# Loading the convolution's image by upper and lower halves, in pieces of ten full rows, in place of halves by columns

## The reference, cut to what matters

```python
h = einsum('oc,bchw->bohw', w1, x)          # 48 -> 288 channels ("expand")
h = relu(bn(h, g1, b1, m1, v1))
h = conv_3x3_depthwise(h, wd, padding=1)    # each channel by itself
h = relu(bn(h, gd, bd, md, vd))
h = einsum('oc,bchw->bohw', w2, h)          # 288 -> 48 ("project")
h = bn(h, g2, b2, m2, v2)
return x + h
```

## Time and profile before

| what | us |
|---|---|
| median of 3 runs | 2143.0 (2142.28, 2143.00, 2147.72) |
| the profiled execution | 2147.49 |
| its span, first to last instruction | 2145.7 |
| attention | to about 855 |
| MLP | about 856 to 1220 |
| convolution | about 1220 to the end |

### The profile page before, as it was taken

How to read it: one execution, slowest core, us unless ns; L and a number is a source line. 1 busy time by engine, 2 the same in 40 slices (tenths; PEclk the granted TensorE clock), 3 DMA queues, 4 the chain that set the end, 5 groups by cost and what they waited for, 6 DMA issues and landing times.

```text
span 2145.7 us, 75224 instructions
## 1 busy us (share of the span) xinstructions
PE 2012.5 (94%) x29192; PEld 1624.2 (76%) x29192; DVE 1464.3 (68%) x2586; ACT 1368.1 (64%) x2839; POOL 673.1 (31%) x874
## 2 busy tenths in 40 slices
PE   5999999999999997689999799998999899999996
PEld 4777777777777776445555489888989888888985
DVE  4899999998999997545555555554655556565553
ACT  2777777777777775456666466665666566665664
POOL 3233323333233332903200243343333332425240
PEclk9999999999999998799999899999999999999999
DMA  1222222222222221566655262635444445445331
GB/s 59 63 67 69 66 69 70 67 69 66 69 70 66 69 67 63 118 153 152 149 134 133 60 142 70 128 85 117 111 102 111 109 83 136 91 116 111 90 98 31
DMA packets 286411, 198.71 MB, mean 93 GB/s; under 512 B 225975, under 2 KB 275656, under 8 KB 276472
## 3 DMA queue, kind: packets, MB, share of 16 engines
q1 hardware_dynamic: 282850, 189.17, 35.1%
q0 software_dynamic: 2336, 6.20, 1.2%
q10 hardware_dynamic: 1014, 0.34, 0.1%
HBM read 128.31 MB, written 54.72 MB: 85 GB/s over the span
## 4 chain that ended last, share of the span: by engine, by line
PE 53%; ACT 2%; DVE 2%; issue 1%; DMA 1%; SPq 0%; ACTq 0%; DVEq 0%
PE psum L1063 13%; PE psum L1082 12%; PE psum L1115 9%; PE psum L664 6%; PE psum L649 5%; PE psum L1123 5%; PE psum L638 3%; ACT h2T L1151 1%; DMA room<-tok_mid 1%; DVE h L848 0%; DVE room L680 0%; SPq L600 0%; ACT h L847 0%; DVE room L848 0%; DVE room L693 0%
## 5 line engine op out<-in xcount | busy, mean ns | idle before, releaser
L897 POOL TENSOR_TENSOR mats<-mats,dscale 112x2048 f32<-112x2048 f32 x72 | 260.8, 3622 | 483.4 <-DMA mats<-in_taps 480.5
L1063 PE MATMUL psum<-ew,xp 64*100 64x96 f32 x6144 | 318.3, 251 | 24.6 <-DVE h L848 11.1
L1151 ACT ACTIVATE h2T<-psum 96x1024 f32<-96x1024 f32 x192 | 195.7, 1019 | 202.4 <-PE psum L1123 202.4
L848 DVE TENSOR_SCALAR h<-psum 100x384 f32<-100x384 f32 x384 | 211.8, 557 | 155.7 <-PE psum L1063 138.7
L1063 PEld LDWEIGHTS psum<-ew,xp 64*100 64x100 f32 x6144 | 290.8, 165 | 34.6 <-DVE h L848 15.8
L1082 PE MATMUL psum<-h,mats 128*64 128x128 f32 x4608 | 273.1, 278 | 11.7 <-issue 10.1
L1082 PEld LDWEIGHTS psum<-h,mats 128*64 128x64 f32 x4608 | 256.8, 139 | 21.2 <-issue 12.1
L847 ACT ACTIVATE room<-psum 64x512 f32<-64x512 f32 (+1 forms) x384 | 206.1, 537 | 93.6 <-PE psum L1082 87.2
L344 PE MATMUL psum<-kb,qa 128*64 128x256 f32 x2048 | 251.7, 388 | 2.2 <-DMA kb<-kk 2.2
L848 DVE TENSOR_SCALAR room<-psum 64x512 f32<-64x512 f32 (+1 forms) x288 | 174.2, 605 | 80.5 <-PE psum L1082 74.6
L1115 PE MATMUL psum<-h2T,pw 128*64 128x128 f32 x3072 | 209.2, 278 | 17.7 <-ACT h2T L1151 17.7
(11 more groups left out here) (155 smaller groups left out, 3436.8 us busy)
## 6 DMA issues: line engine op xcount, KB each, us to landing
mats<-in_taps SPq DMA_DIRECT2D x69, 896.0 KB, 6.2
tok_mid<-mid SPq DMA_DIRECT2D x128, 224.0 KB, 1.9
room<-tok_mid SPq DMA_DIRECT2D x64, 448.0 KB, 3.7
piece<-img_mid SPq DMA_DIRECT2D x196, 63.8 KB, 2.4
img_mid<-room SPq DMA_DIRECT2D x128, 97.5 KB, 2.7
kb<-kk SPq DMA_DIRECT2D x512, 24.0 KB
out<-yc SPq DMA_DIRECT2D x32, 384.0 KB, 4.3
scratch<-in_x_tokens SPq DMA_DIRECT2D x126, 96.0 KB, 1.9
```

The lines of the kernel that those rows point to most:

```text
L848: return nc.vector.tensor_scalar(dst, src, 0.0, None, ALU.max)
L897: nc.gpsimd.tensor_tensor(m, m, bc(scale[0:MROWS, at:at + TCH], 2, POUT), ALU.mult).then_inc(mats_scaled, 1)
L1063: mm = nc.tensor.matmul(ring[(j + u) % 4][0:PIN, p:4 * CH:4], xp[hx][rows, 2 * j + p, :], w1[rows, c, :], start=True, stop=True)
L1151: nc.scalar.activation(h2T[n % 2][0:CH, :, :], ps_t[0:CH, :, 0:POUT * PART], ACT.Copy).then_inc(copied, 1)
```

## The change

The image is halved by rows: a half is 64 full rows, its upper 32 on partitions 0 to 47 and its lower 32 on partitions 64 to 111. `PC, PR = 16, 4` (now for each side) gives the same 64 patches a side. A piece is ten full rows of 130 columns, so each channel's part is one run of 5200 bytes, and there are four pieces and eight DMAs a half, in two slots. A cut writes 16 patches. The borders are cleared on all partitions by three memsets. A step's eight patches lie beside one another, so the add into `y` writes eight runs of eight pixels in eight rows. `y` is 32 rows of 128 pixels and lies in `room`. It is stored to an output that is in image order already. The last layer's bias comes in as a row of `w2` against a row of ones in `h2T`, so `c2` goes with its loads and folding; its loads for `b` and `m` are made for `q`. The tiles' total work in multiplications is the same. The diff, cut:

```diff
-PC, PR = 8, 16
-PATCHES = PC * PR
+PC, PR = 16, 4
+PATCHES = 2 * PC * PR
 MROWS = 112
-HALF = PC * PW
-SC = HALF + 2
+ROWS = PH * PR
...
-        q = {n: sb(f"q_{n}", [CH, C]) for n in "gvt"}
-        c2 = {n: sb(f"c_{n}", [P, 1]) for n in "gbmvt"}
+        q = {n: sb(f"q_{n}", [CH, C]) for n in "gbmvt"}
...
-        SLOTS = 5
-        SIDE = HALF // 2 + 2
+        SLOTS = 2
...
-        piece = [sb(f"piece{s}", [P, PH + 2, SIDE]) for s in range(SLOTS)]
+        piece = [sb(f"piece{s}", [P, PH + 2, W + 2]) for s in range(SLOTS)]
...
-        y = sb("yc", [P, PR * PH, PC // 2 * PW])
+        y = room[:, PATCHES // 2 * CH:PATCHES // 2 * CH + ROWS * W].rearrange("q (r x) -> q r x", x=W)
+        mark = sb("mark", [1, 1])
...
-        STEPS = [(pc, a, PART) for a in range(0, PR, PART) for pc in range(PC // 2)]
+        STEPS = [(j, c) for j in range(PR) for c in range(0, PC, PART)]
...
-            slot, _ = place_of(j)
-            src = piece[slot][:, :, :]
-            src = bass.AP(src.tensor, src.offset, [list(src.ap[0]), [PW, PC // 2], [SIDE, PH + 2], [1, PW + 2]])
-            dst = xp[hx][:, :, :].rearrange("k (c j) (r x) -> k j c r x", j=PR, x=PW + 2)[:, j]
+            src = piece[j % SLOTS][:, :, :]
+            src = bass.AP(src.tensor, src.offset, [list(src.ap[0]), [PW, PC], [W + 2, PH + 2], [1, PW + 2]])
+            dst = xp[hx][:, PC * j:PC * j + PC, :].rearrange("k c (r x) -> k c r x", x=PW + 2)
...
         def close_borders(pool, hx, h):
...
-            if hx == 0:
-                last = nc.gpsimd.memset(ones(0)[:, 0, :, :, 0], 0.0)
-            else:
-                last = nc.gpsimd.memset(ones(1)[:, PC // 2 - 1, :, :, PW + 1], 0.0)
-            last.then_inc(border_set, 1)
-            pool.wait_ge(border_set, 2 * h + 1)
-            for r in range(2):
-                nc.gpsimd.memset(ones(r)[:, :, 0, 0, :], 0.0)
-                last = nc.gpsimd.memset(ones(r)[:, :, PR - 1, H - PH * (PR - 1) + 1:, :], 0.0)
-            last.then_inc(border_set, 1)
+            at = xp[hx][:, :, :].rearrange("k (j c) (r x) -> k j c r x", c=PC, x=PW + 2)
+            edge = at[0:ONE, 0, :, 0, :] if hx == 0 else at[ONE:P, PR - 1, :, PH + 1, :]
+            for n, t in enumerate((at[:, :, 0, :, 0], at[:, :, PC - 1, :, PW + 1], edge)):
+                nc.gpsimd.memset(t, 0.0).then_inc(border_set, 1)
+                pool.wait_ge(border_set, 3 * h + n + 1)
...
+        def load_piece(eng, b, hx, j, done):
+
+            for r in range(2):
+                top = 2 * ROWS * hx + ROWS * r + PH * j - 1
+                lo, hi = max(top, 0), min(top + PH + 2, H)
+                eng.dma_start(piece[j % SLOTS][ONE * r:ONE * r + C, lo - top:hi - top, :], d["img_images"][:, b, lo:hi, :])\
+                    .then_inc(done, 16)
...
-            constants = [(t[...], 0.0) for t in (w1, w2, *c2.values(), *h2T, *piece, *xp)]
+            constants = [(t[...], 0.0) for t in (w1, w2, *h2T, *piece, *xp)]
             constants += [(t[96:P, :, :], 0.0) for t in mats]
+            constants += [(t[CH:P, :, :], 1.0) for t in h2T]
...
-            loads += [(q[n][:, :], d[f"bn2_{n}"].partition_broadcast(CH)) for n in "gv"]
-            loads += [(c2[n][r:r + C, :], d[f"bn2_{n}"].rearrange("(c a) -> c a", a=1)) for n in "gbmv" for r in (0, ONE)]
+            loads += [(q[n][:, :], d[f"bn2_{n}"].partition_broadcast(CH)) for n in "gbmv"]
             loads += [(dn[n], d[f"{n}d"].partition_broadcast(MROWS)) for n in "vgmb"]
-            assert len(loads) == 24
+            assert len(loads) == 18
...
-            nc.gpsimd.memset(y[:, 0:H // 2, :], 0.0).then_inc(y_stored[0], 32)
-            pool.wait_ge(y_stored[0], 32)
-            nc.gpsimd.memset(y[:, H // 2:H - PH, :], 0.0).then_inc(y_done, 1)
-            pool.wait_ge(y_done, 1)
-            nc.gpsimd.memset(y[:, H - PH:H, :], 0.0).then_inc(y_stored[1], 32)
-            pool.wait_ge(y_stored[1], 32)
+            for n, (done, value) in enumerate(((y_stored[0], 32), (y_stored[1], 32), (y_done, 1))):
+                nc.gpsimd.memset(mark[:, :], 0.0).then_inc(done, value)
+                pool.wait_ge(done, value)
...
-                slot, nth = place_of(j)
-                wait(pool, cut, nth)
-                lo, hi, off = piece_rows(j)
-                for r in range(2):
-                    pool.dma_start(piece[slot][ONE * r:ONE * r + C, off:off + hi - lo, :],
-                                   d["img_images"][:, 0, lo:hi, HALF // 2 * r:HALF // 2 * r + SIDE]).then_inc(first_loaded, 16)
+                wait(pool, cut, j - SLOTS + 1)
+                load_piece(pool, 0, 0, j, first_loaded)
...
-            nc.scalar.activation(c2["t"][:, :], c2["v"][:, :], ACT.Sqrt, bias=eps[:, :]).then_inc(root, 1)
...
+            nc.vector.tensor_tensor(w2[CH:CH + 1, CHUNKS - 1, 0:C], q["b"][0:1, :], q["m"][0:1, :], ALU.subtract)
+            for t in (e, dn):
...
             def load_half(b, hx, h):
 
                 for j in range(PR):
-                    slot, nth = place_of(j)
-                    wait(sp, cut, PR * h + nth)
-                    lo, hi, off = piece_rows(j)
-                    for r in range(2):
-                        x0 = HALF * hx + HALF // 2 * r
-                        sp.dma_start(piece[slot][ONE * r:ONE * r + C, off:off + hi - lo, :],
-                                     d["img_images"][:, b, lo:hi, x0:x0 + SIDE]).then_inc(piece_loaded[slot], 16)
+                    sp.wait_ge(cut, PR * h + j - SLOTS + 1)
+                    load_piece(sp, b, hx, j, piece_loaded[j % SLOTS])
...
-                        rows = slice(PH * PART * block, PH * PART * (block + 1))
+                        rows = slice(ROWS // 2 * block, ROWS // 2 * (block + 1))
                         for r in range(2):
-                            sp.dma_start(d["out"][4 * b + 2 * hx + r].rearrange("c (y x) -> c y x", y=H)[:, rows, :],
+                            at = 2 * ROWS * hx + ROWS * r
+                            sp.dma_start(d["out"][b].rearrange("c (y x) -> c y x", y=H)[:, at + rows.start:at + rows.stop, :],
...
             def add(n, b, hx, c, k):
 
-                pc, a, m = STEPS[n]
+                j, first = STEPS[n]
                 dve.wait_ge(y_ready, NSTEP * k + n + 1)
-                rows = slice(PH * a, PH * (a + m))
-                cols = slice(PW * pc, PW * pc + PW)
-                dst = y[:, rows, cols]
-                src = ps_y[n % 2][:, 0:POUT * m].rearrange("q (r x) -> q r x", x=PW)
+                view = lambda t: t.rearrange("q (p r x) -> q p r x", p=PART, x=PW)
+                dst = y[:, PH * j:PH * j + PH, PW * first:PW * (first + PART)].rearrange("q r (p x) -> q p r x", x=PW)
+                src = view(ps_y[n % 2][:, :])
                 if c == 0:
                     if n % PER_BLOCK == 0:
                         dve.wait_ge(y_stored[n // PER_BLOCK], 32 * (2 * b + hx) + 32)
-                    p0 = PR * pc + a
-                    x = xp[hx][:, p0:p0 + m, :].rearrange("k j (r x) -> k j r x", x=PW + 2)[:, :, 1:PH + 1, 1:PW + 1]
-                    nc.vector.tensor_tensor(dst.rearrange("q (j r) x -> q j r x", j=m),
-                                            src.rearrange("q (j r) x -> q j r x", j=m), x, ALU.add).then_inc(y_done, 1)
-                elif c == CHUNKS - 1:
-                    nc.vector.scalar_tensor_tensor(dst, src, c2["b"][:, 0:1], dst, ALU.add, ALU.add).then_inc(y_done, 1)
+                    x = xp[hx][:, PART * n:PART * n + PART, :].rearrange("k p (r x) -> k p r x", x=PW + 2)[:, :, 1:PH + 1, 1:PW + 1]
+                    nc.vector.tensor_tensor(dst, src, x, ALU.add).then_inc(y_done, 1)
                 else:
                     nc.vector.tensor_tensor(dst, src, dst, ALU.add).then_inc(y_done, 1)
...
-    d["out"] = nc.dram_tensor("out", (B * 4, C, H * HALF // 2), F32, kind="ExternalOutput").ap()
+    d["out"] = nc.dram_tensor("out", (B, C, H * W), F32, kind="ExternalOutput").ap()
     block_program(nc, d)
     got = run_bass_kernel_spmd(nc, [arrays], core_ids=[0]).results[0]["out"]
-    return got.reshape(halves).transpose(0, 3, 4, 1, 2, 5).reshape(B, C, H, W)
+    return got.reshape(B, C, H, W)
```

More of the change, by code:

```diff
@@ L788, in conv @@
         LEAD = 3
-        BLOCKS = PR // PART
+        BLOCKS = 2
         PER_BLOCK = NSTEP // BLOCKS
@@ L801, in more @@
             return not (hx == 1 and isinstance(b, int))
[L803 to L817, removed]
+        FIXED = 2 + 2 + SLOTS + 2 + LOADS + 2 + 2 + 2 * SLOTS
+        PER_SLOT = PR // SLOTS
         def number(b, hx, c):
@@ L955, in _ @@
                 for j in range(PR):
-                    slot, _ = place_of(j)
-                    pool.wait_ge(piece_loaded[slot], 32 * (PER_HALF[slot] * (h - 1) + nth_in_slot(j) + 1))
-                    if j:
-                        pool.wait_ge(cut, PR * h + j)
-                    else:
-                        pool.wait_ge(border_set, 2 * h)
+                    pool.wait_ge(piece_loaded[j % SLOTS], 32 * (PER_SLOT * (h - 1) + j // SLOTS + 1))
```

(16 more changed lines are left out.)

13 lines of the change are left out of this document (2 added, 11 removed).

## The result

The changed kernel took 2162.2 us in the median of 5 runs (2158.3 to 2166.1), against 2143.2 for the kernel before: a ratio of 1.0084, with an interval of 1.0064 to 1.0104. It is 18 us slower by the ratio and 19 by the medians, where 2 us less was forecast, and 2162 lies above the range of 2134 to 2149. The profiled execution took 2158.3, a span of 2156.5, so the two traces differ by 10.8 us: the execution profiled before was near the slow end of its runs, this one at the fast end. I read the places from the traces and the size from the medians.

What follows compares the result with a forecast made beforehand. TensorE, busy for 94% of the span, was taken to bound the kernel. Terms of -1.0, -0.06, -0.5, -0.2 and -0.2 made -2.0, from a median of 2143.0 to 2141.0 us, range 2134 to 2149.

Steps and rivals of the forecast that it cites:

- the term "-1.0" for the transfers of the pieces: First chunks of halves that load pieces: fewer, longer transfers shorten TensorE's waits slightly, -1.0 us.
- -4.7 (or -8.0): Lower bound for piece transfers: first chunks fall to the last half's excess of 1.13 us; -8.0 includes h6.
- rival 2: First chunks of halves that load pieces: long runs hold up PE's instruction loads, +8.3 us, 2150; chance 0.10.
- Rival 1: First chunks: the piece packets are the stall, so these fall to the last half's level, -8.0 us, 2134; chance 0.10.
- Rival 3: MLP's start: the crowd of loads dissolves, token wait and slow stretch vanish, -8.1 us, 2133; chance 0.06.
- the term of -0.2 for POOL's loads: MLP's start: six small loads fewer, tap loads about 1.4 us sooner, same bytes; -0.2 us, bounds -8.1 and +2.
- Rival 4: Piece transfers: not shortened, as 48 runs are handled worse than 112, but hidden; 2142 us, chance 0.06.
- The signs that I had named: Whole kernel: some 120,000 fewer small packets, quiet chunks 36.36, h6's wait near 2 us, cuts 2.1 us, no POOL waits.
- rival 2's sign: First chunks of halves: above 40 us with a granted clock under 1.00.
- The constants at the MLP's start: POOL's memsets before the MLP: the second xp memset ends 0.6 us earlier; -0.5 us taken, bounds -0.8 and +0.5.
- SP, POOL, adds, bias: Convolution: SP and POOL cost 0 on the path, bias nothing, only the very last add counts, -0.06 us.

Runs made afterwards that it cites:

- its best version: Changed kernel with late pieces, taps and stores of y in four DMAs each, POOL's two early tap loads behind the first half's cuts: 2133.4 us, 0.9938.

## Why the prediction was wrong

**The step that failed** is the term "-1.0" for the transfers of the pieces; it is about +18, which is what the medians give back when the pieces come late (2165.1 to 2147.0), or 16 by the ratios. Its bounds were -4.7 (or -8.0) on one side and rival 2 on the other, which ends at 2150. In its place the runs showed: dummy loads alone bring the 18 us, leaving the pieces out takes them away, and the wait is PE's, put down to "issue", behind an instruction packet that comes late. Rival 2 had the place (first chunks of the halves that load pieces), the sign and the means (PE's instruction loads), but my price, each odd half raised to h6's excess, was too low, and it named the wrong property: long runs. Neither ten times shorter runs (2169) nor DMAs of a tenth of the bytes (2155) cure it.

**What misled me** was right as far as it went. I read that h6's wait came when no piece packet had moved, and concluded that most of the stall belongs to taps and store. That is right for h6: with split taps its excess goes from 4.4 to 0.4, with the pieces late only to 3.3. For h1 and h3 it is not: either change alone nearly clears them, so their stall took both (the changed kernel without pieces keeps 0.9 and 0.8 us there). And even "the old pieces have no part in the old stall" wouldn't say that the new ones add nothing to it. PE already waited in each first chunk, so there was no slack left there, and any new traffic at that place goes straight onto the path. I had counted the pieces' engine time, 14.1 against 8.4 us a half, which did fall (384 runs of 365 ns are 8.8); what counts here is what the engines hold at the moment when a load is due. Then 0.65 MB were queued at once before (ten DMAs) and 1.0 MB after (four DMAs of 250 KB), and half the queue or smaller DMAs each bring back some 9 us.

**Rival 1** (2134, the piece packets are the stall) didn't come: the transfers got shorter and the stall longer, and without any pieces the time is only that of the kernel before. As a reading of the old trace it holds for h1 and h3 in part, and not for h6. **Rival 3** went the other way. In the profiled execution the waits for tokens were 3.28 and 2.89 us, 6.2 in all for 5.8, but in the other 12 traces with the changed kernel's MLP they were 10.6 to 12.3, against 5.8, 7.1 and 9.5 in the three of the kernel before and its versions. The convolution starts at 1234.8 to 1236.3 us in these three and at 1235.7 to 1240.6 in the 13, at 1239.0 in the middle one. So the term of -0.2 for POOL's loads, bounded at +2, is by these traces nearer to +4. The version with late pieces, 0.8 us above before in the median, leaves little room for as much in the medians, and why the same two tap loads, issued at nearly the same time, make PE wait longer there stays open. **Rival 4** is wrong as well; the transfers did get shorter.

**The signs that I had named** were mixed. Quiet chunks of 36.36, h6's wait near 2 us (1.85), and no wait of PE for POOL came as said; the cuts were quicker (1.56 us for 2.1). The small packets fell by 109,472, between the two marks (100,000 and 120,000). Of rival 2's sign, first chunks above 40 with a clock under 1.00, h3 and h6 had both halves, h5 only the length.

**The constants at the MLP's start** came out as forecast. The timeline of POOL and of DVE there, to be held against the earlier trace rows:

```profile
858.68 2.42 POOL L895 MEMSET piece<- 128x1300 f32 x2
861.16 10.92 POOL L895 MEMSET xp<- 128x6400 f32 x2
...
865.75 6.44 DVE L679 TENSOR_SCALAR room<-room 48x192 f32<-48x192 f32 x2 [4.90 <-DMA room<-in_fc_b]
```

POOL's memsets end at 872.08 instead of 872.34, in a trace where they begin 0.2 us later (855.93 for 855.72), so that stretch is 0.47 us shorter; DVE's two scalings took 6.44 us instead of 6.96, for -0.5 forecast.

**SP, POOL, adds, bias**: costed at nothing, and nothing was measured; quiet chunks stayed at 36.36 and PE waits for POOL nowhere in the convolution. **The rule on packets** from the Trainium skill ("DMA: Bandwidth & Descriptors", "Queues, rings and completion order"), by which an engine serves a whole packet before it turns to another queue, gave the right sign where I gave it no weight. That smaller tap DMAs cure the stall at equal bytes agrees with it (2134.6 for 2147.7). It doesn't explain that ten DMAs do hardly better than five and that half the queue helps at equal DMA size, and runs of 520 bytes in place of 5200 bring nothing back (2169.2 for 2165.1), which by my use of the rule they should.

**What stays open** is how size of a DMA and bytes in the queue share the rest: splitting also stretches the issue over time, which thins out the queue, so the two were never fully apart. For the taps the length of the runs changed with it. The trace shows the instruction packet late, but not behind which transfer, or on which engine, it waited.

## What to carry to other kernels

A transfer that nobody waits for can still cost time: where an engine's program is long and its instruction loads come through the same DMA engines, look at which moments it waits for "issue", hold the instruction queue's packets against them, and keep large transfers away from them or cut those that stand there. One wait on the issuing queue was worth 18 us here by the medians, and splitting 896 KB loads in four was worth 11 to 13 us in the kernel before, 14 to 16 in the changed one and 7 to 10 where the pieces were late, by ratios and by medians. Fewer, longer, cheaper DMAs are only better if they don't arrive together in front of something that is due. The whole change brought no gain that these runs show: its best version is within the noise of the kernel before with split taps.

## What was not expected of the hardware

Four loads of 250 KB a half with no reader cost 18 us of a 2147 us kernel through waits that the profile calls "issue" (2.99 us in one chunk). The lower clock came with some of these waits and not with others: in the changed kernel 0.96 over the chunk of h3 (3.30 us) and 0.92 over that of h6 (1.85), but 1.00 over that of h1 (2.98). Runs of 520 bytes moved at 9.8 bytes a ns for each engine, hardly faster than 136-byte ones at 9, while 5200-byte runs made 14. GpSimd's cut of 1600 columns took 1559 ns where 400 columns took 528, three times for four times the work.
